# Self-attention inside a decoder layer: reciprocal ahead of three rotations, normalisation one batch earlier, masks ahead of powers, third value projection between transposes

## The reference, cut to what matters

```python
q = (X @ WQ + bQ).reshape(B, T, H_TOT, DH).transpose(0, 2, 1, 3)
q = rope(rms_norm(q))
v = (X @ WV + bV).reshape(B, T, H_TOT, DH).transpose(0, 2, 1, 3)
k = rope((X @ WK + bK).reshape(B, T, N_SH, DH).transpose(0, 2, 1, 3))
k = jnp.tile(k, (1, N_BR, 1, 1))
scores = jnp.einsum('bhqd,bhkd->bhqk', q, k)
denom = jnp.sqrt(jnp.sum(k * k, axis=-1))[:, :, None, :]
w = scores / denom
...
w = w * full_mask
sinks = jnp.broadcast_to(jnp.tanh(sink_scalars).reshape(1, H_TOT, 1, 1), (B, H_TOT, T, 1))
probs = jax.nn.softmax(jnp.concatenate([w, sinks], axis=-1), axis=-1)
out = jnp.einsum('bhqk,bhkd->bhqd', probs[..., :T], v)
...
y = ctx @ WO + bO
return y.mean(axis=1)
```

## Time and profile before

| | |
|---|---|
| time, three runs | 2591.87 us median (2591.48 to 2596.62) |
| the profiled execution | 2596.9 us, span 2595.1 us |
| PE busy in the span | 2147.9 us (83%) |
| DVE busy | 1987.7 us (77%) |
| POOL busy | 1275.2 us (49%) |
| ACT busy | 1272.3 us (49%) |
| granted TensorE clock, mean | 0.915 |

### The profile page before, as it was taken

One profiled execution on the slowest core, in us unless ns is written; L12 is line 12 of the kernel. 1 busy time (PEld: TensorE's weight loads), 2 busy tenths in 40 slices (PEclk: granted clock), 3 DMA queues, 4 the chain that ended last, 5 costly groups with the idle time before them and its releaser, 6 DMA issues. The chain is left out here.

```text
span 2595.1 us, 54503 instructions
## 1 busy us (share of the span) xinstructions
PE 2147.9 (83%) x19760; PEld 1691.8 (65%) x19760; DVE 1987.7 (77%) x3663; ACT 1272.3 (49%) x2464; POOL 1275.2 (49%) x1473
## 2 busy tenths in 40 slices
PE   2787878787885479898899888898899889898976
PEld 1555555555562367777777777777777777777764
DVE  4666665657542169998988989889889898898995
ACT  3232323232320257666666566566566566656653
POOL 2464545545442145555555454555455455545543
PEclk9899999999987789999999898899899889989997
DMA  5000000000004300100000000000000010001000
GB/s 170 8 20 10 19 9 19 9 19 9 16 8 145 92 18 16 30 19 20 25 25 16 20 23 26 20 19 24 27 16 19 20 30 19 20 16 34 6 8 10
DMA packets 41511, 70.29 MB, mean 27 GB/s; under 512 B 4638, under 2 KB 21166, under 8 KB 41260
## 3 DMA queue, kind: packets, MB, share of 16 engines
q1 hardware_dynamic: 35868, 56.31, 7.1%
q0 software_dynamic: 3632, 7.58, 1.2%
q10 hardware_dynamic: 1760, 3.28, 0.5%
HBM read 60.54 MB, written 9.86 MB: 27 GB/s over the span
## 5 line engine op out<-in xcount | busy, mean ns | idle before, releaser
L1346 DVE MATCH_REPLACE8 ca_W<-ca_top,ca_W 128x722 f32<-128x722 f32 (+1 forms) x624 | 554.0, 896 | 0.0
L1334 DVE MAX8 ca_top<-ca_W 128x8 f32<-128x722 f32 (+1 forms) x624 | 537.8, 900 | 1.2
L949 POOL TENSOR_TENSOR ca_S<-ca_S,ca_W 128x722 f32<-128x722 f32 (+1 forms) x208 | 357.2, 1737 | 262.3 <-ACT ca_W L1208 262.3
L88 PE MATMUL ca_pS<-ca_KH,ca_QH 128*128 128x362 f32 (+1 forms) x384 | 156.3, 407 | 139.2 <-ACT ca_S L1225 131.7
L926 POOL TENSOR_TENSOR ca_KL<-ca_K,ca_KH 128x384 fp32r<-128x384 f32 (+1 forms) x128 | 114.3, 893 | 310.8 <-ACT ca_KH L1200 308.4
L1324 DVE MAX8 ca_top<-ca_S 128x8 f32<-128x722 f32 (+1 forms) x208 | 180.8, 902 | 111.1 <-ACT ca_S L1225 96.3
L1230 ACT ACTIVATE ca_PT<-ca_pT 128x768 f32<-128x768 f32 (+1 forms) x208 | 164.0, 788 | 182.4 <-PE ca_pT L1081 181.5
L88 PE MATMUL ca_pF<-ca_cH,ca_WkH 128*128 128x338 f32 (+1 forms) x512 | 199.0, 389 | 23.3 <-POOL ca_cL L934 23.3
L1114 PE MATMUL ca_pO<-ca_PT,ca_V 128*32 128x56 f32 (+5 forms) x4608 | 217.3, 225 | 0.0
L364 POOL TENSOR_TENSOR sa_ss<-sa_ss,sa_minus_half 100x16 f32<-100x16 f32 x64 | 191.1, 2994 | 22.3 <-DVE sa_ss L534 22.2
L1208 ACT ACTIVATE ca_W<-ca_W,ca_shift 128x722 f32<-128x722 f32 (+1 forms) x208 | 185.8, 893 | 22.8 <-DVE ca_W L1346 22.8
(11 more groups left out here) (213 smaller groups left out, 5231.7 us busy)
## 6 DMA issues: line engine op xcount, KB each, us to landing
ca_raw<-in_ctxT SPq DMA_DIRECT2D x32, 384.0 KB, 3.4
ca_raw<-in_ctxT SPq DMA_DIRECT2D x32, 338.0 KB, 3.1
sa_xin<-in_x SPq DMA_DIRECT2D x16, 200.0 KB
sa_xres<-in_x SPq DMA_DIRECT2D x16, 200.0 KB
x_scratch<-sa_x SPq DMA_DIRECT2D x16, 200.0 KB
x_scratch<-y_scratch POOLq DMA_DIRECT2D x16, 200.0 KB, 13.0
ca_xin<-x_scratch SPq DMA_DIRECT2D x16, 200.0 KB
ca_x<-x_scratch SPq DMA_DIRECT2D x16, 200.0 KB
```

The source lines that it names most:

```text
L88: pe.matmul(out, ah, bh, start=start, stop=False)
L949: pool.tensor_tensor(S[k][rows, :], S[k][rows, :], W[r][rows, :], ALU.subtract).then_inc(p_ready, 1)
L1334: n_of[t.i] = order.mark(dve.max(top[r][rows, 8 * k:8 * k + 8], W[r][rows, :]))
L1346: ins = dve.match_replace(W[r][rows, :], eight, W[r][rows, :], REMOVED)
```

## The change

Five edits in `self_program`; no arithmetic is added or removed.

1. DVE takes the reciprocal before rotations 1, 2 and 3. Before them stand bias 3, squares 2 and 3 and the layer-norm statistics.
2. Statistics, their power and the normalisation are those of the batch after the next (`far`), so that `xn` is ready a body earlier. There is one more call of the body at the start (At(-2)). The normalisation stands between rotations 2 and 3.
3. POOL makes the four masks with only power 0 between them; powers 1, 2 and 3 follow, then the power of the statistics.
4. On TensorE `turn(0)` comes before `value(2)`, and on ACT the copy of that value lies between the first and the second high part. The transposes use the banks 1, 1, 0, 1 and not 1, 0, 1, 0, with the waits that follow from it.
5. DVE makes the first low part before the products of the previous batch.

```diff
-        v_bank, qk_bank, hT_bank = (lambda br: br % 2), (lambda n: n % 2), (lambda g: (g + 1) % 2)
+        v_bank, qk_bank, hT_bank = (lambda br: br % 2), (lambda n: n % 2), (lambda g: (1, 1, 0, 1)[g])
...
-            body(At(-1), cur=False, prev=False, nxt=True)
...
+            body(At(-2), cur=False, prev=False, nxt=False, far=True)
+            body(At(-1), cur=False, prev=False, nxt=True, far=True)
...
-                if nxt:
-                    need(sp, xn_ready, b.count(1, 1))
-                    sp.dma_start(xin[:, :], batch_of(A["x"], b, 1)).then_inc(x_in, 16)
+                if far:
+                    need(sp, xn_ready, b.count(1, 2))
+                    sp.dma_start(xin[:, :], batch_of(A["x"], b, 2)).then_inc(x_in, 16)
...
+                if cur:
+                    mask(0)
+                    mask(1)
                 if nxt:
-                    pool.wait_ge(var_ready, bn.count(1, 1))
+                    power(0)
+                if cur:
+                    mask(2)
+                    mask(3)
+                if nxt:
+                    for n in range(1, QB):
+                        power(n)
+                if far:
+                    pool.wait_ge(var_ready, b.next(2).count(1, 1))
                     pool.tensor_tensor(rstd[:, :], mv[:, 1:2], minus_half[:, 0:1], ALU.pow).then_inc(rstd_ready, 1)
...
-                if cur:
-                    value(2)
                 for g in range(QC // 4):
+                    if cur and g == 1:
+                        value(2)
...
+                if cur:
+                    low(0)
                 if prev:
 
                     dve.wait_ge(num_mm, b.count(HK, 0))
...
+                    biased(0)
+                    biased(1)
+                    squares(0)
+                    biased(2)
+                    squares(1)
+                    rope(0)
+                    biased(3)
+                    squares(2)
+                    squares(3)
+                if far:
+                    statistics()
...
                 if cur:
                     dve.wait_ge(den_mm, b.count(HK, HK))
                     dve.reciprocal(rden[:, :], pq[:, 3, 0:T]).then_inc(rden_ready, 1)
+                if nxt:
+                    rope(1)
+                    rope(2)
+                if far:
+                    normalised()
+                if nxt:
+                    rope(3)
...
                     pe.wait_ge(roped, b.count(QB, g + 1))
-                    if g < 2:
-                        pe.wait_ge(v_ready, b.count(NL, 2 + g))
+                    if g == 0:
+                        pe.wait_ge(v_ready, b.count(NL, 2))
+                    elif g == 2:
+                        pe.wait_ge(v_ready, b.count(NL, 3))
                     else:
-                        pe.wait_ge(hT_lo, b.count(QC // 4, g - 1))
+                        pe.wait_ge(hT_lo, b.count(QC // 4, (g + 1) // 2))
...
                 if cur:
+                    turn(0)
                     pe.wait_ge(v_ready, b.count(NL, 1))
                     value(2)
-                    turn(0)
                     turn(1)
```

More of the change, by code:

```diff
@@ L335, in _, with body @@
             one = pool.to_reg(1.0)
-            def body(b, cur, prev, nxt):
+            def body(b, cur, prev, nxt, far):
                 bn = b.next()
-                if nxt:
-                    pool.wait_ge(var_ready, bn.count(1, 1))
-                    pool.tensor_tensor(rstd[:, :], mv[:, 1:2], minus_half[:, 0:1], ALU.pow).then_inc(rstd_ready, 1)
[L342 to L364, removed]
@@ new lines, in mask @@
+                def mask(g):
+                    pool.wait_ge(e_ready, b.count(NH, 4 * g + 4))
+                    order.mark(pool.tensor_tensor(step[:, :], minus_half[0:1, 0:1], minus_half[0:1, 0:1], ALU.mult))
+                    for br in LIVE:
+                        high, low = BRANCHES[br]
+                        part = E[0:T, 4 * g:4 * g + 4, br, :]
+                        windows = [(-low, 1)] + ([(high - 1, -1)] if high < T else [])
+                        for base, sign in windows:
+                            order.after(order.n)
+                            ins = pool.affine_select(
+                                out=part, in_=part, compare_op=ALU.is_ge, fill=one, base=base,
+                                pattern=[[0, 4], [sign, T]], channel_multiplier=-sign)
+                            if (g, br, sign) == (NH // 4 - 1, LIVE[-1], windows[-1][1]):
+                                ins.then_inc(masked, 1)
+                            else:
+                                order.mark(ins)
@@ L479, in rope, with statistics, normalised, low @@
                     order.after(order.n)
[L481 to L482 removed]
+                def statistics():
+                    dve.wait_ge(x_in, b.next(2).count(16, 16))
                     row_stats(dve, order, xin[:, :], stats[:, :], mv[:, :], var_ready)
[L484 to L485 removed]
+                def normalised():
+                    need(dve, xT_mm, b.count(1, 2))
+                    dve.wait_ge(rstd_ready, b.next(2).count(1, 1))
                     dve.tensor_scalar(xn[:, :], xin[:, :], mv[:, 0:1], rstd[:, :],
                                       ALU.subtract, ALU.mult).then_inc(xn_ready, 1)
+                def low(g):
+                    dve.wait_ge(hT_hi, b.count(QC // 4, g + 1))
+                    dve.tensor_tensor(qkTl[:, 4 * g:4 * g + 4, :], heads(pp[:, hT_bank(g), 0:4 * T], 4),
+                                      qkTh[:, 4 * g:4 * g + 4, :].bitcast(F32), ALU.subtract).then_inc(hT_lo, 1)
+                def biased(n):
+                    dve.wait_ge(qk_mm, bn.count(QB, n + 1))
+                    dve.tensor_tensor(qk[:, D * n:D * n + D], pp[0:T, qk_bank(n), :],
+                                      bias_qk[:, D * n:D * n + D], ALU.add).then_inc(qk_ready, 1)
+                def squares(n):
+                    part = ss[:, NH * n:NH * n + NH]
+                    dve.wait_ge(sq_ready, bn.count(QB, n + 1))
+                    ins = dve.tensor_reduce(part, seg(rq, n), AX.X, ALU.add)
+                    if n < NL:
+                        then(ins)
+                        ins = dve.tensor_scalar(part, part, 1.0 / DH, RMS_EPS, ALU.mult, ALU.add)
+                    ins.then_inc(ss_ready, 1)
+                if cur:
+                    low(0)
                 if prev:
@@ L499, in body @@
                 if cur:
[L500 to L503, removed]
+                    for g in range(1, QC // 4):
+                        low(g)
                 if nxt:
```

44 lines of the change are left out of this document (17 added, 27 removed).

## The result

The change makes the kernel faster: 2556.95 us median (2554.59 to 2558.24, 4 runs) against 2594.22 us (2591.48 to 2596.62, 4 runs). The ratio is 0.9856, with a 95% interval of 0.9839 to 0.9873, so 37 us. Forecast were 51 us, 2541 us, in a range of 2519 to 2563.

The account below looks back on a forecast made before the run. DVE's two rotations ahead of the reciprocal, stalling PE, bound the 44.48 us batch. Arcs 17.4 + 17.55 + 5.16 = 40.1 us, plus 1.0 for the clock, give 41.1; 15 x 3.38 = 50.7 us saved: 2541 us, range 2519 to 2563.

Parts of the forecast that it names:

- Which stall goes: PE's idle times per batch, 5.29 us for the reciprocal and 1.26 us for the fourth mask, would both go.
- The masks on DVE: Scores to value projection 1: two rotation 0 instructions slowed 0.34 us each by selects, 16.93 us becoming 17.55.
- that rival: Masks block DVE for whole selects in rotation 0: 2.2 us and not 0.68, 42.6 a batch, 2564 us; chance 0.06.
- What comes behind the reciprocal: Reciprocal to scores: rotations now stand ahead of the low parts, transposes and WO, 17.4 us where it was 14.63.
- The whole ring: One batch's cycle, reciprocal to scores to value projection 1 to next reciprocal: 40.1 us without clock change, from 44.48.
- The clock: Thin PE stretch between value(2) and WO lowers the clock in about two batches of three: 1.0 us a batch.
- The rival of a clock low through WO and more: Clock low through WO, scores and first projections in each batch: 43.4 us a batch, 2576 us; chance 0.10.
- Its own signs: Profile signs: prediction wrong if scores start under 16.5 or over 20 us after the reciprocal; WO takes 3.6 to 5.2.
- the first arc: The part of a batch from the reciprocal to the first scores: 14.63 us before, forecast 17.4 without the clock term.
- Its other sign: Prediction wrong if value projection 1 starts over 18.5 us after the scores.
- The sum: Self-attention loop: 41.1 us a batch, 3.38 less than 44.48, over 15 passages 50.7 us; start and end within 1 us.
- the forecast's own range: Whole kernel, 2530 to 2556 us, from a clock term of 0.3 to 1.57 a batch and masks 0 to 1.02.

Follow-up runs that it names:

- the dense matmuls: Changed kernel plus 14 extra 512-column matmuls, results unread, in PE's gaps between value(2) and turn(1) and between turn(2) and turn(3): 2536.83 us.
- thin ones: Changed kernel plus 14 extra matmuls of 16 columns instead of 512 in the same PE gaps: 2570.15 us.
- the reciprocal late: Changed kernel with the reciprocal put back behind rotation 3, all else as changed: 2588.20 us.

## Why the prediction was right in kind and off in size

- **Which stall goes.** Right. The reciprocal starts 0.33 us after the first numerator matmul (400.19 to 400.52), as forecast, the 5.29 us and the 1.26 us are gone, and the arc from value projection 1 to the reciprocal is 5.37 us (437.26 to 442.63, the next reciprocal) for a forecast of 5.16.
- **The masks on DVE.** Right: rotation 0 is 4.32 us and not 3.67, two instructions of three at 0.34 more; scores to value projection 1 is 17.50 us (419.76 to 437.26) for a forecast of 17.55. No instruction waited for a whole select, and that rival falls.
- **What comes behind the reciprocal.** Right: 9.63 us to the first low part for a forecast of 9.65. At the full clock, with the dense matmuls, the arc to x1 is 17.55 us; scores start 0.2 earlier, so 17.35 for 17.4. The whole ring without a change of clock was forecast at 40.1 us and is 40.15.
- **The clock.** The step that failed in size, in the words of the prediction: "I take the fall in about two batches of three, 1.0 us a batch". It falls in every batch and costs 42.44 less 40.15, 2.3 us. `turn(3)` takes 0.69 us until WO starts and not 0.37, and WO takes 1.58 us more in one batch (5.18) and 2.71 more in the next (6.31). Two things were missed. I priced the fall by one WO of 5.17 us; but in every other batch the low level lasts for nearly all of WO. And I took a stretch a little busier than the one in the earlier trace rows (1.22 us of 4.0 against 0.94 of 3.5) to be spared in a third of the batches; none was. The rival of a clock low through WO and more, at 43.4 us a batch, was nearer to the measured 42.44 than the forecast's 41.1; by the median it was 19 us off and the forecast 16. What happened lies between the two: WO paid more than the forecast had, but the scores behind it ran at the upper level (0.41 us for the first four at 419.76 and at 463.00, as in the earlier trace rows).
- **Its own signs.** The prediction called itself wrong if the scores start more than 20 us after the reciprocal. They start 19.24 us after it in one batch (400.52 to 419.76) and 20.37 in the next (442.63 to 463.00), and WO's 6.31 is above its 5.2. So in every other batch the first arc fails by the prediction's own sign, and that by the clock alone. Its other sign, value projection 1 later than 18.5 us after the scores, did not come.
- **The sum.** The 14 passages of the rows give 622.68 less 594.16, 28.5 us. The prediction added a fifteenth at the same price and let the start and the end keep their length within 1 us. But the first x1 comes 5.3 us earlier (122.82 for 128.09) and the last passage is 1.2 us longer (29.82 for 28.64), which makes 32.6; the forecast was 50.7. The missing 18 us are 20 of the clock's term (1.34 a batch) less 2 that start and end gave beyond the fifteenth passage. Those 2 us, and some 6 in the parts that were not changed, were luck. The median of 2556.95 lies just outside of the forecast's own range of 2530 to 2556, and inside the wide one. The low end of the own range does not follow from its bounds either: with a clock term of 0.3 and no price for the masks the sum is 2521.
- **The Trainium skill's pages.** The Trainium skill (TensorE: Matmul & The Clock Gate, "HAM oscillation") says that gaps between bursts of matmuls bring the throttle back each time. Its example has waits for transfers, in which PE does nothing, while here PE does transposes between gaps of at most 2.31 us. So the page does not settle this case by itself, and the prediction read it more widely than it is written. That every batch paid is what the traces show. The Trainium skill (SBUF — State Buffer, "Who interferes with whom") says that the second of two contending instructions blocks until the first is done; the contention is there, but it costs 0.34 us for each, less than a select, and the measurement decides.

Which edits carry it, at the clock as it falls: the reciprocal first is necessary (without it 44.43 us a batch) and not sufficient (alone 44.19). At the full clock, by the kernels with dense matmuls, it is 43.08 before, 41.96 with the reciprocal first and 40.15 with all edits. So it gives 1.1 us and the others 1.8, of which the first low part ahead of the products is 1.1 by the run without it (that one at the clock as it falls). The masks' order and the order of the transposes show next to nothing (42.58 and 42.22 a batch without them, for 42.44), but both were undone only where the clock falls in each batch, and the last section shows that 1 us can vanish there. What the early normalisation gives was not measured; it was not undone by itself.

## What to carry to other kernels

Before an engine's idle stretch is taken away, look at where PE will be thin afterwards and which dense work comes next: here the fall of the clock moved from 48 short matmuls, where it cost 1.4 us a batch, to a dense projection, where it costs 2.3, and took a third of the gain. Whether a slow stretch is one of waits or of the clock, a handful of dense matmuls in the gaps tells in one run, with thin ones as the control. And an engine that now waits ahead of the critical instruction is room to fill: moving one rotation there took off 49 us, where the whole change took off 37. Some 1.9 us a batch of that are there at the full clock (40.15 to 38.22, both with dense matmuls); the other 1.7 are that the clock now holds in most batches.

## What the runs showed that I had not expected

Three kernels with different waits run at the same time a batch inside the loop: 44.37 us before, 44.37 with the reciprocal first alone (arcs of 22.75 and 21.63), 44.37 to 44.39 with the reciprocal late (29.99 and 14.38). The changed kernel alternates between 42.1 and 43.2. With dense matmuls in the gaps the kernel before, the one with the reciprocal first alone and the changed kernel have values of their own (43.07, 42.10, 40.21); the one with the reciprocal late was not run so. So where the clock falls in each batch, the loop settles in a pattern in which a change of one arc by 1 or 2 us can vanish from the time. That the clock's fall does this is shown for the first two kernels, which differ by 1.0 us when it is kept up and not at all when it falls; how it comes to the same value was not taken apart.
